# Cross-attention and feed-forward on one core: the layer norm in front of q reduced to a scaling, its mean folded into Wq

## The reference

```python
q = split_heads(layernorm(x) @ Wq.T + bq)      # 16 heads of 8; this layer norm has no gain and no bias
k = split_heads(ctx @ Wk.T + bk)
v = split_heads(ctx @ Wv.T + bv)
score = einsum('bhij,bhkj->bhik', k, q) / sqrt(8)
attn = softmax(score, axis=1)                   # over the heads
x = x + (attention output) @ Wo.T + bo
x = x + ffn(layernorm(x))                       # three residual blocks, each: linear with a low-rank part,
                                                # layer norm, gelu, linear
```

## Time and profile before

| | |
|---|---|
| median of three runs | 391.69 us (391.21 to 392.34) |
| profiled execution | 390.71 us |
| its span, first to last instruction | 388.9 us |
| mean granted TensorE clock | 0.98 |
| busy: TensorE, VectorE, ScalarE, GpSimd | 346.2, 331.9, 291.4, 282.3 us |

### The profile page before, as it was taken

One profiled execution on the slowest core, in us unless ns is written; L12 is line 12 of the kernel. 1 busy time (PEld: TensorE's weight loads), 2 busy tenths in 40 slices (PEclk: granted clock), 3 DMA queues, 4 the chain that ended last, 5 costly groups with the idle time before them and its releaser, 6 DMA issues.

```text
span 388.9 us, 13057 instructions
## 1 busy us (share of the span) xinstructions
PE 346.2 (89%) x4772; PEld 252.7 (65%) x4772; DVE 331.9 (85%) x817; ACT 291.4 (75%) x575; POOL 282.3 (73%) x337
## 2 busy tenths in 40 slices
PE   2768699999999999999979786879899999999974
PEld 1335456776677667766756664756678877887863
DVE  4655999999999999999998989669989998987752
ACT  3456778887888888888866544447989899989862
POOL 6460888898889888988887878766777777774221
PEclk9978999999999999999999998999999999999999
DMA  5747555685586557755661400000011001111111
GB/s 151 185 134 217 163 172 157 202 235 160 153 227 196 180 151 202 229 171 148 184 192 55 137 3 0 2 3 1 3 51 32 27 27 54 29 29 29 53 56 54
DMA packets 53121, 43.28 MB, mean 111 GB/s; under 512 B 4496, under 2 KB 46944, under 8 KB 53088
## 3 DMA queue, kind: packets, MB, share of 16 engines
q1 hardware_dynamic: 53088, 42.84, 37.7%
HBM read 26.05 MB, written 16.78 MB: 110 GB/s over the span
## 4 chain that ended last, share of the span: by engine, by line
PE 55%; DVE 23%; issue 9%; POOL 7%; ACT 4%; DMA 1%; POOLq 0%; DVEq 0%; ACTq 0%
PE score_ps L1073 8%; PE att_ps L1039 7%; PE score_ps L975 5%; PE wo_ps L927 5%; DVE zsum L618 5%; DVE negmax L597 5%; DVE st L641 4%; PE score_ps L964 3%; POOL probs L397 3%; PE work L993 3%; PE work L1131 2%; PE work L997 2%; PE score_ps L1139 2%; PE score_ps L1067 2%; PE att_ps L1139 2%
## 5 line engine op out<-in xcount | busy, mean ns | idle before, releaser
L397 POOL TENSOR_TENSOR probs<-probs,rz 128x1024 f32<-128x1024 f32 x64 | 135.9, 2140 | 32.5 <-DVE rz L621 32.1
L433 POOL TENSOR_TENSOR rs<-ve,minus_half 128x4 f32<-128x4 f32 (+1 forms) x50 | 59.3, 1187 | 48.4 <-DVE ve L563 35.4
L721 ACT ACTIVATE probs<-score_ps 128x1024 f32<-128x1024 f32 x64 | 65.6, 1025 | 21.4 <-PE score_ps L975 21.1
L597 DVE TENSOR_REDUCE negmax<-score_ps 128x64 bf16<-128x1024 f32 x64 | 75.4, 1177 | 6.0 <-PE score_ps L964 5.9
L618 DVE TENSOR_REDUCE zsum<-probs 128x64 f32<-128x1024 f32 x64 | 77.3, 1208 | 2.1 <-ACT probs L721 2.1
L1073 PEld LDWEIGHTS score_ps<-lin_t,h 128*128 128x128 f32 x320 | 38.3, 191 | 17.2 <-DVE h L680 15.8
L816 ACT ACTIVATE z<-score_ps,rs 128x128 f32<-128x128 f32 x160 | 45.8, 382 | 2.3 <-POOL rs L433 2.3
L1039 PE MATMUL att_ps<-probs,v_diag 128*32 128x64 f32 x2048 | 44.3, 226 | 2.9 <-POOL probs L397 2.7
L975 PE MATMUL score_ps<-negmax,ident_bf 128*128 128x512 bf16 x128 | 39.5, 391 | 8.2 <-DVE negmax L597 8.2
L927 PEld LDWEIGHTS wo_ps<-wo_t,att_t 128*128 128x128 f32 x256 | 37.8, 195 | 13.8 <-issue 12.2
L1073 PE MATMUL score_ps<-lin_t,h 128*128 128x128 f32 x320 | 42.9, 281 | 4.2 <-DVE h L680 1.8
(11 more groups left out here) (177 smaller groups left out, 690.8 us busy)
## 6 DMA issues: line engine op xcount, KB each, us to landing
q_parts<-parts SPq DMA_DIRECT2D x16, 512.0 KB, 3.6
q_stack<-q_parts SPq DMA_DIRECT2D x64, 128.0 KB, 3.2
k_stack<-k_parts SPq DMA_DIRECT2D x32, 256.0 KB, 3.4
ctx_sb<-in_ctx SPq DMA_DIRECT2D x16, 256.0 KB, 3.7
k_parts<-parts SPq DMA_DIRECT2D x16, 256.0 KB, 3.0
out<-x_all SPq DMA_DIRECT2D x16, 256.0 KB, 2.3
x_all<-in_x SPq DMA_DIRECT2D x14, 256.0 KB, 3.8
x_all<-in_x SPq DMA_DIRECT2D x1, 512.0 KB, 6.0
```

What stands on the lines that cost most here:

```text
L397: nc.gpsimd.tensor_tensor(e[:, :, :, :], e[:, :, :, :], by_query.broadcast_to([P, BANDS, SEQ, ADJ]), ALU.mult).then_inc(s_probs, 1)
L433: nc.gpsimd.tensor_tensor(rs2[v][:, lo:hi], ve2[v][:, lo:hi], minus_half[:, lo:hi], ALU.pow).then_inc(p_rs[v], 1)
L597: nc.vector.tensor_reduce(negmax[p % 2][:, :], score_ps[p % 2][:, :].rearrange("p (h k) -> p k h", k=SEQ), AX_X, ALU.max, negate=True).the ...
L721: nc.scalar.activation(probs[p][:, :, :, :], score_ps[p % 2][:, :].rearrange("p (u s k) -> p u k s", s=ADJ, k=SEQ), ACT.Exp, scale=SCALE). ...
```

## The change

The mean of a token is no longer subtracted from x. Since `sum_d (x_d - mean) * Wq[o, d]` equals `sum_d x_d * (Wq[o, d] - mean over d of Wq[o, :])`, the row means are taken from Wq instead, once. The reciprocal deviation comes as its half (`half_rstd`), so Wq is doubled as well. Three VectorE operations at the head of its queue, ahead of the first `bn_stats`, build `wq_c`; TensorE transposes that in place of Wq. GpSimd loses four operations per chunk, and ScalarE's `xln` becomes a Copy with a per-partition scale and no bias. It waits for `s_rstd` instead of `s_nmr`.

```diff
@@ gpsimd, chunk, p == 1
-                        nc.gpsimd.tensor_tensor(agg[:, 0, :], stats[:, :, 1], stats[:, :, 4], ALU.add)
                         nc.gpsimd.tensor_tensor(agg[:, 1, :], stats[:, :, 2], stats[:, :, 5], ALU.add)
...
                         nc.gpsimd.tensor_tensor(agg[:, 3, :], agg[:, 2, :], agg[:, 2, :], ALU.mult)
-                        nc.gpsimd.tensor_scalar(neg2mean[:, :], agg[:, 0, :], -1.0, None, ALU.mult)
...
                         nc.gpsimd.tensor_tensor(half_rstd[:, :], veps4[:, :], minus_half[:, 0:TPC],
                                                 ALU.pow).then_inc(s_rstd, 1)
-                        pool.wait_ge(s_rstd, c + 4)
-                        nc.gpsimd.tensor_tensor(nmr[:, :], neg2mean[:, :], half_rstd[:, :], ALU.mult)
-                        nc.gpsimd.tensor_scalar(rstd[:, :], half_rstd[:, :], 2.0, None, ALU.mult).then_inc(s_nmr, 1)
@@ vector, after neg_ident
+            dve.wait_ge(s_qk_load, 16 * 2)
+            nc.vector.tensor_reduce(wq_sum[:, :], w_in["q"][:, :], AX_X, ALU.add).then_inc(s_wq, 1)
+            dve.wait_ge(s_wq, 1)
+            nc.vector.tensor_scalar(wq_mean[:, :], wq_sum[:, :], -2.0 / D, None, ALU.mult).then_inc(s_wq, 1)
+            dve.wait_ge(s_wq, 2)
+            nc.vector.tensor_scalar(wq_c[:, :], w_in["q"][:, :], 2.0, wq_mean[:, :], ALU.mult, ALU.add).then_inc(s_wq, 1)
@@ scalar, normalised_input
-                        act.wait_ge(s_nmr, k + 1)
+                        act.wait_ge(s_rstd, k + 1)
...
-                            ins = nc.scalar.activation(xln[:, t, :], x_all[:, k, t, :], ACT.Identity,
-                                                       bias=nmr[:, t:t + 1], scale=rstd[:, t:t + 1])
+                            ins = nc.scalar.activation(xln[:, t, :], x_all[:, k, t, :], ACT.Copy,
+                                                       scale=half_rstd[:, t:t + 1])
@@ tensor
-            for i, k in enumerate("qk"):
-                nc.tensor.transpose(bank[i][:, 0:P], w_in[k][:, :], ident[:, :]).then_inc(s_tr, 1)
+            pe.wait_ge(s_wq, 3)
+            nc.tensor.transpose(bank[0][:, 0:P], wq_c[:, :], ident[:, :]).then_inc(s_tr, 1)
+            nc.tensor.transpose(bank[1][:, 0:P], w_in["k"][:, :], ident[:, :]).then_inc(s_tr, 1)
```

More of the change, by code:

```diff
@@ L88, in build @@
         lb_in = sb("lb_in", [P, NLIN, RANK])
+        wq_sum = sb("wq_sum", [P, 1])
+        wq_mean = sb("wq_mean", [P, 1])
+        wq_c = sb("wq_c", [P, P])
         w_t = {k: sb("w_t_" + k, [P, P]) for k in "qkv"}
@@ L119, in build @@
         agg = sb("agg", [P, 4, TPC])
-        neg2mean = sb("neg2mean", [P, TPC])
         veps4 = sb("veps4", [P, TPC])
         half_rstd = sb("half_rstd", [P, TPC])
-        rstd = sb("rstd", [P, TPC])
-        nmr = sb("nmr", [P, TPC])
         xln = sb("xln", [P, TPC, D])
@@ L164, in build @@
         s_wperm = sem("s_wperm")
+        s_wq = sem("s_wq")
         s_split = sem("s_split")
@@ L186, in build @@
         s_rstd = sem("s_rstd")
-        s_nmr = sem("s_nmr")
         s_xln = sem("s_xln")
```

## The result

Fifteen runs of the changed kernel have a median of 387.33 us (385.94 to 390.63), fifteen of the kernel before, beside them, 391.10 us (389.86 to 392.34). The ratio is 0.9933, 95% interval 0.9907 to 0.9959: faster, by 0.67% (the two medians by themselves lie 1.0% apart). The profiled execution took 388.33 us with a span of 386.5 us, against 390.71 and 388.9 before: 2.4 us less. I compare these two executions first and come back to the spread of the runs, which is wider than the gain (4.7 us after, 2.5 before).

The account below looks back on a forecast made before the run. TensorE, busy 89% of the span, was taken as the bound, with VectorE close behind at 85%. Terms -0.7, -0.2 and -0.7 sum to -1.6 us, giving 390.1 us from the 391.69 median; 8-in-10 range 388.4 to 392.1.

Parts of the forecast that it names:

- that of 200 us: Near 200 us: scalings on GpSimd run earlier, L575 is no longer held, the next maximum starts sooner; -0.7 us.
- that of chunk 0: Chunk 0 and 1: GpSimd 0.84 us earlier frees TensorE, but VectorE limits the gain; -0.2 us, bounds 0 and -0.5.
- the -0.7 of the opening: Opening: v_diag memsets and first scores come 0.7 us earlier although chunk 0 is 0.65 later; bounds -1.2 and 0.
- The head of the opening: Start of the kernel: Wq operations delay the first statistics by 2.1 us; the first xln ends 0.65 us later.
- The memsets: Opening: v_diag memsets on GpSimd hold L536, which the feed-forward weights need; they start 0.7 us earlier, at 22.5.
- TensorE's clock gives more: Rival, opening and 204 to 206 us: shorter idle, more work at the upper clock, 1.5 us less, 388.6 us; chance 0.16.
- VectorE then sets the pace: Chunk 0: with TensorE freed, VectorE, having only 0.3 us of air per chunk, limits the gain to -0.2 us.
- Chunks 2 to 11: Steady middle of the attention: savings hidden behind TensorE, so 0 us, bounds -0.5 and +0.3.
- The slower rival: Opening: clock stays low some 3 us more, past 33 us; +3.3 us, net +1.7, 393.4 us; chance 0.09.

Follow-up runs that it names:

- e2: Changed kernel with xln as Identity with two per-partition operands (bias a column of zeros) instead of Copy; 387.93 us, ratio 0.9944 to the kernel before.
- e4: Changed kernel with the four small GpSimd operations put back only in the normalisation during chunk 0, results unused; 388.01 us, one run.
- e5: Changed kernel with the wait and three Wq operations behind the first bn_stats in VectorE's queue; 385.21 us, ratio 0.9858 to the kernel before.
- e3: Changed kernel with the four small GpSimd operations put back only in the normalisation at chunk 12, results unused; 386.68 us, one run.
- e1: Changed kernel with the four small GpSimd operations put back in every chunk, results unused, xln waiting for the last; 391.93 us, 1.0028 of the kernel before.
- e6: Kernel before with only the three Wq operations added at the head of VectorE's queue, result unused; 392.63 us, ratio 1.0042 to the kernel before.
- e8: Changed kernel with ten unused bf16 matmuls in TensorE's idle time before the feed-forward weights in the opening; 387.35 us, ratio 0.9899 to the kernel before.
- e13: Changed kernel with unused matmuls in three places: ten in the opening, eight in chunk 13, seven in chunk 15; 387.12 us, ratio 0.9908 to the kernel before.
- e10: e5 with the first of two v_diag memsets moved ahead of the third normalisation on GpSimd; 385.95 us, ratio 0.9899 to the kernel before.

## Why the prediction was right, and where it was off

- **Sign and size.** Forecast -1.6 us on the profiled execution; it was -2.4. The forecast time of 390.1 compares with 391.69 x 0.9933 = 389.1 by the ratio; the median itself, 387.33, lies below the range's low end of 388.4. The places and the chain from one engine to the next held. Of the terms, that of 200 us was right, that of chunk 0 too small, one near 270 us was missing, and the -0.7 of the opening came out by luck: only 0.2 of it came by the path that the prediction describes. By that path alone the four steps are -0.2, -0.8, -0.7 and -0.3, together -2.0 us.
- **The head of the opening.** Statistics forecast at 5.6, started at 5.70; first xln from 8.9 to 10.0 forecast, 9.10 to 10.38 measured. Three small misses add up to the 0.5 us by which the second xln ended too late: the statistics started 2.22 us later instead of 2.1, GpSimd's chain gave 0.84 us instead of 0.95, and each xln group took 1.28 us, not 1.15, twice. One Copy takes 391 ns, as the 382 of L816 let expect, but four in a row from SBUF overlap less than L816's from PSUM do (four of those take 1.13 to 1.17 us from the first start to the last end), and these are the rows the 1.15 came from. The form's row:

```profile
L733 ACT ACTIVATE xln<-x_all,half_rstd 128x128 f32 x40 | 12.7, 391 | 0.0
```

  The Trainium skill, "ScalarE: Activation LUTs", What ACT_TABLE_LOAD costs, has 93 ns for each per-partition operand; by it 482 would become 389, and the trace agrees (391). The estimate of 0.37 us for four, worked out from that page's figure, is the measured difference (1.65 against 1.28), and would have been the better term.
- **The memsets.** That L536 (now L538) ends with them was right. They came at 23.04 and not at 22.5, since xln ended 0.64 later than before and not 0.15; so of the term of -0.7 only 0.2 came this way. The other 0.5 came from TensorE's clock, which was back 2 us sooner. That is what the rival *TensorE's clock gives more* says, but its reason does not hold up: the idle time did shrink from 3.76 to 2.47 us (2.4 forecast), yet e2, e4 and e5, with 2.78 to 3.11, had nothing of it, and e3, with 3.27, had more. The first scores at 31.31 (31.3 forecast) were right by luck, by an error and an execution that cancel. The second exp then kept only 0.47, because the second scores waited for ScalarE's eviction of `lin_t`, which I had not looked at.
- **Chunk 0.** The failed step: "VectorE then sets the pace", which left -0.2. e4 measured -0.8. VectorE did fill up: from 45.95 us its row sum, reciprocal and maximum follow one another without a gap, and the maximum moved only 0.2 us more than the exps ahead of it. What the step had wrong is who waits for it. The next exp stands behind TensorE's product, its scores and its subtraction, and these behind GpSimd's scaling; the maximum at 47.66 is for a later one and was done in time. So the 0.8 us went through to the exps, and no later chunk took them back (-1.28 at the fifth exp, -1.40 at the 46th).
- **Chunks 2 to 11.** 0 forecast; with chunk 1 the measured step is -0.1 (-0.3 in e3, e4 and e5). GpSimd's and ScalarE's saving there is hidden, and so is its loss in e1 and e2.
- **Near 200 us.** -0.7 forecast, -0.70 measured, by the steps given: L572's successor held to the end of the second scaling, L575's free, the maximum next. e3 puts it back. The Trainium skill, "SBUF — State Buffer", Who interferes with whom, has a VectorE instruction with two SBUF inputs wait for a GpSimd one that reads SBUF; the 2.10 us, 1.68 us and 0.15 us agree with it.
- **Near 270 us.** -0.3 that I did not see. GpSimd's idle 0.45 us at this place is there in the three kernels with the four operations in every chunk (before, e1, e6) and is 0.14 us in all the others, e3 and e4 with the four in one chunk included. So it goes with them, although the last of them ran 70 us earlier; what makes GpSimd stand still there is not shown.
- **The clock.** The rival had 0.16 and was partly right. Between the two medians lie 3.8 us, between the two profiles 2.4. The runs of the changed kernel fan out by their mean clock, from 385.94 us at 0.985 and 386.2 at 0.989 to 390.63 at 0.973. So some of the medians' difference may be fewer or shorter falls; in the kernel before the relation is loose (of 25 runs, seven at 0.983 took 392.4 to 392.8 us and two at 0.976 took 390.8 and 391.0). That the shorter idle times (2.47, 2.07) bring it is not shown, and two things speak against it: the opening, as above, and the same 2.07 us near 200 us, which ended in a fall in "after" and in none in e2.
- **The slower rival** (a clock that stays low over 33 us) did not come in "after"; in e2 it did in part (until past 32 us) and cost 0.5 us of the 1.23.

## What to carry to other kernels

A saving on an engine with slack was worth nothing here in the steady stretch, and nearly its full length where the pipe was filling or two engines met: 16 savings of 0.8 us on GpSimd moved the end by some 3.3 us, and 0.4 more by the clock of one execution. Preparatory work costs by where it stands in its queue, above all if it brings a wait: 0.75 us of sums cost 2 us ahead of the first statistics, and behind them e5, with four runs, was 2.1 us faster by the medians for the same work. And look at the clock of two profiles before comparing their ends: here one fall is worth 0.7 to 2.4 us, and the change gave 2.4 between the profiles. A run that has the same program up to the place in question shows how much of a step is only the execution.

## What the runs showed of the hardware that I had not expected

- The granted clock fell at up to four places of the same kernel family (the opening, near 204 us, between 230 and 246 us, the last step from 376 us on), and not in every execution. Prices: 1.1 to 2.4 us in the opening ("after", e3 and e4 against e8), 1.5 us near 200 us, 0.7 to 1.2 us in the last step (e13, e6, e8, e10, last two columns of the table); near 240 us, where the kernel before has a fall too, e8 lost 1.6 us and e13 2.7 us more than it. In the last step TensorE had idled 1.32 us before it, in executions with the fall (e8) and without (the kernel before).
- The recorded clock can miss a fall. In the opening of e6 it is 1.00 throughout, while k's product takes 1.91 us, the time it has at 0.50. The durations of like matmuls tell.
- Filling idle time with matmuls kept the clock at 1.00 in that place (idle 0.73 instead of 2.47 us), and a later place fell for longer (e8, e13). That the one brings the other is not shown: e10, without such matmuls, had 0.50 from 230 to 240 us as well. The Trainium skill, "TensorE: Matmul & The Clock Gate", Part 1, has the low clock as the state without activity; the opening of e8 agrees, but no idle time here decides a fall by itself: near 200 us 2.71 us ended with one (before, e1) and without (e3), and 2.06 us with one (e8) and without (e5).
- A VectorE operation that meets two GpSimd instructions back to back was let in between the two scalings of the probabilities (L572, which ends at 198.82 in the middle of the pair; its successor in e3 likewise, after 0.43 us), while the 128x128 multiply of `w_eff` waited out both memsets (3.02 us before, 2.88 in e1, 2.82 in e6). What decides between the two was not tried.
